# First attention of a two-layer transformer kernel: the product with V moves ahead of both first scores in odd units

## What is computed

```
qkv = x @ W_qkv                       # q, k, v: 8 batches, 16 heads, 512 x 8
scores = einsum('bhnd,bhmd->bhnm', q, k) / sqrt(128)
attn = softmax(scores, axis=-1)
out = einsum('bhnm,bhmd->bhnd', attn, v)
x = layernorm(x + out)
```

## Time and profile before

| | |
|---|---|
| median of 3 runs | 1151.23 us (1147.66 to 1152.93) |
| profiled execution, its own time | 1147.96 us |
| its span (first to last instruction) | 1146.2 us, 20697 instructions |
| busy over the span | PE 1050.4 us, DVE 816.2, ACT 761.2, POOL 441.9 |
| L583 maxima, 512 | 322.4 us busy, 684 ns each |
| L396 exponentials, 256 | 252.5 us busy, 1025 ns each |
| L451 first scores, 512 | 176.0 us busy, 412 ns each |
| L524 products, 1024 matmul passes | 137.2 us busy, 608 ns each |
| L511 second scores, 512 | 134.2 us busy, 385 ns each |

### The profile page before, as it was taken

How to read it: one execution, slowest core, us unless ns; L and a number is a source line. 1 busy time by engine, 2 the same in 40 slices (tenths; PEclk the granted TensorE clock), 3 DMA queues, 4 the chain that set the end, 5 groups by cost and what they waited for, 6 DMA issues and landing times. The chain is left out here.

```text
span 1146.2 us, 20697 instructions
## 1 busy us (share of the span) xinstructions
PE 1050.4 (92%) x5936; PEld 498.5 (43%) x5936; DVE 816.2 (71%) x1906; ACT 761.2 (66%) x985; POOL 441.9 (39%) x457
## 2 busy tenths in 40 slices
PE   3999999999999985799999999989999999999796
PEld 1122222222222224577878787763333333322485
DVE  4889999999999917788887789855445444533566
ACT  0067777777777794455555555557888888899553
POOL 0312413214131006366776677574333133310265
PEclk9999999999999996899999999999999999999998
DMA  4453122131221000443334333442422232220001
GB/s 153 134 204 98 57 87 77 47 97 64 80 80 32 1 2 1 140 131 98 97 130 131 120 94 103 137 142 71 151 69 67 85 110 73 64 83 1 1 28 46
DMA packets 74077, 97.16 MB, mean 85 GB/s; under 512 B 12700, under 2 KB 42268, under 8 KB 73628
## 3 DMA queue, kind: packets, MB, share of 16 engines
q1 hardware_dynamic: 74024, 96.51, 27.1%
HBM read 68.29 MB, written 27.79 MB: 84 GB/s over the span
## 5 line engine op out<-in xcount | busy, mean ns | idle before, releaser
L583 DVE TENSOR_REDUCE a_nmax<-a_ps_f 128x1 f32<-128x512 f32 x512 | 322.4, 684 | 39.9 <-PE a_ps_f L451 36.5
L396 ACT ACTIVATE a_prob<-a_ps_s 128x1024 f32<-128x1024 f32 x256 | 252.5, 1025 | 76.2 <-PE a_ps_s L511 74.4
L934 ACT ACTIVATE a_prob<-a_ps_s 128x1024 f32<-128x1024 f32 x256 | 249.1, 1033 | 38.0 <-PE a_ps_s L989 35.0
L1853 POOL TENSOR_TENSOR moe_hl<-moe_hid,moe_hh 128x512 fp32r<-128x512 f32 x136 | 175.8, 1297 | 103.6 <-ACT moe_hh L1745 103.6
L451 PE MATMUL a_ps_f<-a_ks,a_qs 48*128 48x512 bf16 x512 | 176.0, 412 | 29.0 <-DMA a_ks<-parts_k 10.5
L1735 ACT ACTIVATE moe_ps<-moe_ps 128x512 f32<-128x512 f32 x128 | 74.5, 582 | 117.9 <-PE moe_ps L1667 117.2
L451 PEld LDWEIGHTS a_ps_f<-a_ks,a_qs 48*128 48x128 bf16 x512 | 40.2, 94 | 231.3 <-DVE a_nmax L583 190.8
L1002 PE MATMUL a_ps_o<-a_prob,a_va 128*32 128x512 f32 x1024 | 137.2, 608 | 2.5 <-ACT a_osb L922 1.3
L524 PE MATMUL a_ps_o<-a_prob,a_va 128*32 128x512 f32 x1024 | 137.2, 608 | 0.3
L511 PE MATMUL a_ps_s<-a_qs,a_ks 51*128 51x512 bf16 x512 | 134.2, 385 | 3.2 <-ACT a_prob L396 2.9
L1785 DVE TENSOR_TENSOR moe_prod<-moe_cw,moe_ps 128x512 f32<-128x512 f32 x128 | 87.3, 682 | 37.1 <-PE moe_ps L1667 28.8
(11 more groups left out here) (246 smaller groups left out, 1513.5 us busy)
## 6 DMA issues: line engine op xcount, KB each, us to landing
moe_cw<-r_weights SPq DMA_DIRECT2D x256, 128.0 KB, 2.9
parts_q<-a_parts SPq DMA_DIRECT2D x48, 256.0 KB, 2.5
parts_k<-a_parts SPq DMA_DIRECT2D x48, 256.0 KB, 2.5
a_qs<-parts_q SPq DMA_DIRECT2D x128, 96.0 KB, 2.4
a_ks<-parts_k SPq DMA_DIRECT2D x128, 96.0 KB, 2.5
a_xt<-in_x_t SPq DMA_DIRECT2D x8, 256.0 KB, 3.0
out_x<-g_X SPq DMA_DIRECT2D x8, 256.0 KB, 2.3
moe_wg<-in_wg SPq DMA_DIRECT2D x1, 1088.0 KB, 6.4
```

The source lines that it names most:

```text
L396: nc.scalar.activation(prob[:, u % PSLOTS, :, :], ps_s[:, u % 2, :, :], ACT.Exp, scale=float(P) ** -0.5).then_inc(exp_done, 1)
L583: nc.vector.tensor_reduce(nmax[:, half_no, h % 2, col:col + 1], ps_f[:, bank, :], AX.X, ALU.max, negate=True).then_inc(max_done, 1)
L934: nc.scalar.activation(prob[:, u % PSLOTS, :, :], ps_s[:, u % 2, :, :], ACT.Sigmoid, scale=float(HD) ** -0.5).then_inc(exp_done, 1)
L1853: nc.gpsimd.tensor_tensor(hl[:, part_at(j), :], hid[:, hid_at(j), :], hh[:, part_at(j), :], ALU.subtract).then_inc(hl_done, 1)
```

## The change

TensorE's `units` in the first attention tests `not second` in place of `second`. In odd units the product is so issued directly behind the second scores, ahead of score c with its guests; c and d with their guests follow it together. Before it stood between c and d. Nothing else is changed: not the waits of any instruction, the banks, the other engines' orders, nor the second attention.

```diff
@@ -538,7 +538,7 @@
                     if back:
                         s2(b, p, u)
                     for second in range(2):
-                        if second and u % 2 and (back if u > 1 else tail):
+                        if not second and u % 2 and (back if u > 1 else tail):
 
                             if u > 1:
                                 pv(b, p, u // 2 - 1)
```

## The result

The changed kernel takes 1175.24 us (median of six runs, 1173.41 to 1178.98); before it was 1151.2 (six runs, 1147.66 to 1152.93). The ratio is 1.022, with a 95% interval of 1.0196 to 1.0243: slower, by 24 us between the medians, where the forecast of 1170, in a range of 1161 to 1178, had counted 21. The profiled execution took 1173.54 us, its span 1171.8 against 1146.2.

What follows compares the result with a forecast made beforehand. A loop of TensorE and VectorE over three banks was taken as the bound. Pairs summed to 50.44 us a batch against 47.44, over seven batches 21 us: 1169 from the profile, 1172 from the median, forecast 1170, range 1161 to 1178.

Steps and rivals of the forecast that it cites:

- The loop and its steps: First attention, TensorE and VectorE over three banks: the loop's sum per pair of units goes from 2.49 to 2.70 us.
- Score b to the second scores to the product: New end of the loop: b waits for c's maximum, then 0.22 to the second scores and 0.31 to 0.32 to the product.
- plain pair: Two units between successive products with V, eight a batch: forecast 2.70 us each, against 2.49 for the old loop.
- The single pairs: Pairs named by the units of their two products, each given its own forecast length, from 2.70 to 4.07 us.
- 23→25: Pair from unit 23's product to unit 25's, with outputs turned and divided: forecast 4.07 us, before 3.28.
- The total: Seven batches beside which scores run, 3.0 us more each: 21 us; the eighth, from its unit 4 on, nothing.
- The signs: If right: VectorE idle ahead of L583 up some 21 us, same busy sums, span behind the first attention same to 1 us.
- The choice of 1.00: Transposes start 1.00 us behind a product; up to 0.3 earlier was thought possible, 4 us less over 14 pairs.
- The rule weighed: Units 17, 23, 31: one tiling-mode switch fewer would save 2 us by the skill's rule; nothing was counted.
- (a): Rival, faster: VectorE never runs dry, plain pairs cost nothing, 14 us gained, 1134 to 1137 us; chance 0.05.
- (b): Rival, they cancel: big terms (31→1, 23→25, K) come out half as large, leaving 10 us, 1153 to 1157; chance 0.08.
- (c): Rival, the clock gives way: one fall a batch costing about 0.9 to 1.1 us, 7 us in all, 1177; chance 0.07.

Runs made afterwards that it cites:

- The converse order: Product between c and d as before the change, but the odd unit's second scores issued behind c: 1176.24 us, ratio 1.022 to the kernel before.
- the guests' units kept: Product moved ahead of c and d in all odd units but 17, 23 and 31, against the kernel before: 1168.57 us against 1149.69, ratio 1.0154.
- unit 23 alone: Product moved ahead of c and d in unit 23 only, against the kernel before: 1149.77 us against 1150.89, ratio 0.9995.
- the guests ahead: Changed kernel, but in units 17, 23 and 31 the guest is issued ahead of the product, c and d behind it: 1175.39 us, one execution.

## Why the prediction was right

**The loop and its steps.** "Score b to the second scores to the product" was the new wait, and the working gave 2.70 to 2.72 for a plain pair; it is 2.70, by the steps 1.00, 0.42, 0.75, 0.53 of the fence above. The converse order confirms the sum by making the same 2.70 without the move.

**The single pairs** came out as worked: 7→9 3.31 (3.30), 9→11 2.97 (2.99), 11→13 4.01 (4.01), 15→17 2.70 (2.70), 17→19 3.76 (3.80), 31→1 4.06 (4.07). The sum of 50.44 a batch is short by 0.3. Three terms were too small, two others 0.02 and 0.04 too large. 3→5 takes 3.36 for 3.30: the score behind the transposes waits for them and not for d's maximum. 5→7 takes 2.78 for 2.70. And 23→25 takes 4.14 to 4.50 for 4.07: in the old order VectorE still had maxima to do when the transposes ended, here it stands idle, and the division starts late all the same. The two fences are the timeline of TensorE and VectorE in unit 23 of two batches, the second and the fourth:

```profile
149.14 0.66 PE L532 MATMUL a_ps_f<-g_ident,a_osb 128*128 128x128 f32 x4
...
150.28 0.26 DVE L592 RECIPROCAL a_rec<-a_ps_f 128x16 f32<-128x16 f32 x1 [0.93 <-PE a_ps_f L532]
```

```profile
250.83 0.65 PE L532 MATMUL a_ps_f<-g_ident,a_osb 128*128 128x128 f32 x4
...
251.72 0.26 DVE L592 RECIPROCAL a_rec<-a_ps_f 128x16 f32<-128x16 f32 x1 [0.68 <-PE a_ps_f L532]
```

The transposes end at 149.80 and 251.48; the division starts 0.48 and 0.24 later, where I had counted 0.05.

**The total.** Seven batches at the expected length make 21 us. The traces have 22.0 up to the product of unit 3 in the eighth, and 0.6 in the pair 3→5 behind it (3.08 for 2.44), where the transposes now wait 0.56 us for a maximum: the working had put the eighth batch at nothing from its unit 4 on. The other 3.0 us of span lie behind the attention, where the working had named 1 us at most. So the three parts came out 1.0, 0.6 and 3.0 us longer than worked out, none offset another, and the time still lies in the range.

**The signs.** TensorE's clock is 1.00 from 69 to 457 us. The idle time of VectorE ahead of the maxima rose by 16 us and not 21; another 8 stand ahead of the division, which between 60 and 455 us waits 31.3 us for the transposes instead of 23.2. The busy sums of the span moved little, PE 1050 to 1046, DVE 816.2 to 815.6, ACT 761 to 769.

**The choice of 1.00** for the transposes behind a product was right (148.14 to 149.14). That they might start earlier took 4 us off the low end for nothing.

**The rule weighed.** The Trainium skill, TensorEngine Tiling (Array Packing), § Key Properties, has the engine drained when the tiling mode changes; by it I would have counted 2 us less. The kernel that moves the product in units 17, 23 and 31 alone has one change of mode fewer in each than before and takes 0.4 us a batch more. So no saving of that kind shows here; the waits in these pairs are for a bank.

**The rivals.** (a), that VectorE never runs dry, failed on plain pairs, where it runs dry in every one. The gains that it counted on are there (15→17 2.70, 7→9 3.31), as the forecast had them too. (b) failed: no large term came out at half. (c), that the clock gives way, did not decide: in the changed kernel's first attention it is 1.00 from 69 us on. But it does give way in single executions, next.

## What to carry to other kernels

Two engines can pass work through a ring of n buffers: here TensorE fills three banks with scores and VectorE empties them. Such a pair has a loop over each long instruction, here the product. The first item behind it is produced, consumed, and must free its buffer for the item n turns on; when that is the last item ahead of the next long instruction, the round is closed. In plain pairs the second scores added 0.21 us to the round whenever they stood in the gap with the long instruction, and nothing where they stood between a and b. So leave the long instruction alone between two items. In the pairs with guests or the layer norm this wasn't enough to say what an order costs: with the second scores between a and b and the product moved, 9→11 went from 2.49 to 2.89. A period worked out step by step from start-to-start times of one trace held to 0.02 us in plain pairs, while single moves could not be priced one at a time and added up.

## What the runs showed of the hardware that I had not expected

**The clock fell inside the first attention**, where the trace of before had it at 1.00 throughout. In the kernel with the second scores ahead of b and all products moved, the stretches show it, and TensorE's timeline what it cost:

```profile
159.70:163.00 3.30, 3.30 (x16) 0.53 (x8) 2.02 (x5) 2.07 (x3) 0.00 (x0) 0.50 0.00 0
```

```profile
158.76 0.39 PE L451 MATMUL a_ps_f<-a_ks,a_qs 48*128 48x512 bf16 x1 [1.33 <-DVE a_nmax L585]
...
159.38 1.79 PE L524 MATMUL a_ps_o<-a_prob,a_va 128*32 128x512 f32 x8
161.10 0.61 PE L451 MATMUL a_ps_f<-a_ks,a_qs 48*128 48x512 bf16 x2
...
163.03 1.07 PE L524 MATMUL a_ps_o<-a_prob,a_va 128*32 128x512 f32 x8
```

The pair takes 3.65 instead of 2.49: 1.16 us, near the 0.9 to 1.1 that rival (c) had as its price. Ahead of the fall lies the pair 31→1 (4.15 us), in which TensorE was idle for 1.33 us until 158.76; the other batches have the same wait without a fall. A fall happened once in that execution and once behind the first batch in each of three others (the kernels with the guests' units kept, with unit 23 alone and with the guests ahead: 4.46 for 3.30, 3.65 for 2.49 and 4.46 for 3.30), so it is a matter of 1 us an execution and not of each batch. The two kernels with halved maxima have one too, in their first batch (the granted clock falls at 73.4 and 73.7 us), and there TensorE had just been idle for 3.20 and 3.79 us, waiting for a DMA. The Trainium skill, TensorE: Matmul & The Clock Gate, § A second HAM failure mode: psum-queue depth-cycling, describes swings of this kind; here they are rare.

**A late start of the division in unit 23.** How long the division in unit 23 starts behind the end of its transposes differs by batch: 0.13, 0.48, 0.13, 0.23, 0.13 and 0.22 us in the first six. The kernel with three moved products has the same series. Idleness alone doesn't explain it: in unit 31 VectorE is idle too when the transposes end, in all eight batches, and there the division starts 0.04 us behind them, as in unit 23 of the last two. The cause was not tested.
